# Row tiles and quadrants in the edge layers of a graph network kernel, and a node's own term moved out of the first stage

## The reference: two graph layers with residual and layernorm

```python
# first layer, a = node_vec1 (one number per node)
sc_s, sc_v = (xs @ Wsc0) * a/8,  (xv . Wsc1) * a/sqrt(32)      # a node's own term
f_s,  f_v  = (xs @ Wl1_0) * a/8, (xv . Wl1_1) * a/sqrt(32)     # gathered features
h = gelu(edge_attr_8 @ Wfc1 / sqrt(8))                          # [E, 64]
h = gelu(h @ Wfc2 / 8)                                          # [E, 64]
w0, w1, w2, w3 = split(h @ Wfc3 / 8)                            # [E, 192]
gs, gv = f_s[src], f_v[src];  y0, y1 = edge_attr_4[:, 0], edge_attr_4[:, 1:4]
mid = (w0*gs*y0,  w3*(gv . y1)/sqrt3,  (w1*gs) x y1,  w2*gv*y0)
m_s, m_v = segment_sum(mid, dst) / sqrt(32)
alpha = (m_s @ Wa) * a/sqrt(96)
out = (sc_s + alpha*(m_s @ Wl2_s)*a/sqrt(96),  sc_v + alpha*(m_v . Wl2_v)*a/sqrt(96))
x = layernorm(x + out)
```

## Time and profile before

| | us |
|---|---|
| median of 3 runs | 3056.2 |
| lowest and highest | 3023.99 and 3060.04 |
| the profiled execution's own time | 3079.29 |
| its span, first to last instruction | 3077.1 |

### The profile page before, as it was taken

One profiled execution on the slowest core, in us unless ns is written; L12 is line 12 of the kernel. 1 busy time (PEld: TensorE's weight loads), 2 busy tenths in 40 slices (PEclk: granted clock), 3 DMA queues, 4 the chain that ended last, 5 costly groups with the idle time before them and its releaser, 6 DMA issues.

```text
span 3077.1 us, 77590 instructions
## 1 busy us (share of the span) xinstructions
PE 2732.5 (89%) x24164; PEld 2006.0 (65%) x24164; DVE 1638.9 (53%) x4537; ACT 972.3 (32%) x2395; POOL 2004.7 (65%) x1630
## 2 busy tenths in 40 slices
PE   8768777887788888888899999999999999999996
PEld 4334434444444444444588888888888888888983
DVE  3446333443443443433466666666666666666664
ACT  2212212121121211121244444444444444444442
POOL 4555554554555555555188888888888888888884
PEclk5565666556655556665599999999999999999998
DMA  6233332232332332333278888888888887888887
GB/s 191 60 94 92 83 85 76 81 94 77 82 85 78 86 89 80 87 88 81 76 141 140 141 139 140 140 140 140 141 140 141 141 139 140 140 142 143 142 137 176
DMA packets 386447, 354.44 MB, mean 115 GB/s; under 512 B 60080, under 2 KB 337136, under 8 KB 386064
## 3 DMA queue, kind: packets, MB, share of 16 engines
q0 software_dynamic: 150528, 141.40, 31.9%
q1 hardware_dynamic: 231248, 206.49, 24.0%
q10 hardware_dynamic: 4544, 4.93, 0.6%
HBM read 244.83 MB, written 133.44 MB: 123 GB/s over the span
## 4 chain that ended last, share of the span: by engine, by line
PE 75%; another core or an unknown queue 12%; issue 6%; DVE 3%; ACT 2%; SPq 1%; DMA 1%; DVEq 0%; POOL 0%; ACTq 0%; POOLq 0%
PE ps_o L1043 11%; PE ps_w L1031 10%; PE ps_d L1052 8%; PE ps_o L1041 8%; PE ps_x L1065 6%; PE ps_w L894 6%; PE ps_h L887 5%; PE ps_h L882 5%; PE ps_p L838 5%; PE ps_x L1005 3%; PE ps_g L853 2%; PE ps_g L847 1%; PE ps_g L850 1%; PE ps_nd L910 1%
## 5 line engine op out<-in xcount | busy, mean ns | idle before, releaser
L620 POOL DMA_INDIRECT tab<-summed,sidx x784 | 1223.7, 1561 | 285.1 <-issue 229.1
L602 POOL DMA_INDIRECT gat<-f,gidx x784 | 751.8, 959 | 714.3 <-DVE feats L1350 409.6
L1490 DVE TENSOR_TENSOR prod<-ps_w,xg 128x768 f32<-128x768 f32 x392 | 375.5, 958 | 268.6 <-PE ps_w L1031 255.6
L1043 PE MATMUL ps_o<-ro_v,prod 128*128 128x96 f32 x3136 | 479.1, 275 | 0.0
L1043 PEld LDWEIGHTS ps_o<-ro_v,prod 128*128 128x128 f32 x3136 | 414.1, 192 | 0.0
L793 ACT ACTIVATE xg<-ps_x 128x768 f32<-128x768 f32 x392 | 296.4, 808 | 338.2 <-PE ps_x L1065 336.3
L887 PE MATMUL ps_h<-h,w 128*128 128x256 f32 x392 | 225.2, 675 | 178.9 <-issue 106.5
L1031 PE MATMUL ps_w<-hid,wf 64*128 64x128 f32 x4704 | 369.4, 290 | 2.0 <-ACT hid L794 2.0
L1041 PE MATMUL ps_o<-ro_s,prod 96*128 96x96 f32 x1568 | 328.0, 291 | 20.0 <-DVE msg L1501 6.8
L1031 PEld LDWEIGHTS ps_w<-hid,wf 64*128 64x128 f32 x4704 | 294.1, 187 | 70.3 <-issue 44.8
L1052 PE MATMUL ps_d<-msg,same 128*128 128x193 f32 x1568 | 332.3, 334 | 0.7 <-ACT summed L812 0.7
(11 more groups left out here) (259 smaller groups left out, 3330.0 us busy)
## 6 DMA issues: line engine op xcount, KB each, us to landing
xt<-in_src_rows SPq DMA_DIRECT2D x196, 256.0 KB
xt<-feat SPq DMA_DIRECT2D x784, 36.0 KB
xt<-in_ea SPq DMA_DIRECT2D x196, 128.0 KB
feat<-xt SPq DMA_DIRECT2D x25, 576.0 KB
hot_dst<-in_dst_rows SPq DMA_DIRECT2D x98, 128.0 KB
gat<-f,gidx POOLq DMA_INDIRECT x784
hot_dir<-sh_rows SPq DMA_DIRECT2D x98, 128.0 KB
xt<-hot_dst SPq DMA_DIRECT2D x196, 64.0 KB
```

Of the source, the lines that this page charges most:

```text
L602: pool.indirect_dma_start(out=gat[:, r % 4, k, :], out_offset=None, in_=t["f0"], in_offset=bass.IndirectOffsetOnAxis(ap=gidx[:, r // 4, at ...
L620: pool.indirect_dma_start(out=t["tabs"][into[k]], out_offset=bass.IndirectOffsetOnAxis(ap=sidx[:, r, k:k + 1], axis=0), in_=summed[:, r, k ...
L1043: last = pe.matmul(ps_o[:, k, 96 + 64 * c:192 + 64 * c], prod[:, ur % 2, k, 1 + c, :], ro_v[:, c, :], start=True, stop=True)
L1490: dve.tensor_tensor(prod[:, r % 2, :, :, :].rearrange("p k c e -> p k (c e)"), ps_w4[:, :, 0:3 * P], xg[:, r // 2, r % 2 * 2:r % 2 * 2 + 2 ...
```

## The change

Four parts. (1) Layer 1 takes two row tiles: 16 rows at partition 0 and 16 at partition 32, each with 128 columns, into two banks. (2) Layer 2 takes four 64x64 quadrants of 128 columns each, and the gelus are two instructions each; layer 3's order becomes 0, 2, 1, 3. To have the second bank, `ps_p` and both `ps_g` share one bank, and `tile_sums(u)` waits for `acc_done >= u`, the addition of the window sums of the group before. (3) The first stage multiplies by the weights of the gathered features alone, 64 and 96 columns, and DVE's additions are gone from it; the rows of x are loaded by SP, behind `y` and ahead of the first L399. (4) The own term is made in the first layer: two steps before a node tile's update its rows of x are turned (s mod 8 = 3), projected one step later with 64 and 96 columns (s mod 8 = 4), and added by DVE (`add_self`). The 25th tile's is made in step 3. The eight-column attributes lie in 48 rows of 128 columns a group instead of 16 of 256.

```diff
+SELF_LAST = 3
+def self_at(s, lag):
+    if s - lag == SELF_LAST:
+        return NT - 1
+    return tile_at(s, lag - 2, range(NT - 1))
...
-            w1 = sb(c2, "w1", [16, P])
+            w1 = sb(c2, "w1", [48, P])
-            ea8 = sb(c2, "ea8", [16, 2, 256])
+            ea8 = sb(c2, "ea8", [48, 2, P])
...
-            ps_h1, ps_h2 = ps_h[:, 0:256], ps_h[:, 256:512]
+            ps_hy = pb(c2, "ps_hy", [P, 512])
+            ps_h1 = [ps_h[:, 0:P], ps_hy[:, 0:P]]
+            ps_h2 = [ps_h[:, P:2 * P], ps_hy[:, P:2 * P]]
...
-            ps_p = pb(c2, "ps_p", [P, 512])
-            ps_gw = pb(c2, "ps_g", [P, 2, 256])
-            ps_g = [ps_gw[:, i, :] for i in range(2)]
+            ps_pg = pb(c2, "ps_pg", [P, 512])
+            ps_p = ps_pg[:, 0:FEAT]
+            ps_g = [ps_pg[:, FEAT + 4 * WIN * i:FEAT + 4 * WIN * (i + 1)] for i in range(2)]
...
                 for h in range(2):
-                    sp.dma_start(w1[8 * h:8 * h + 8, S * h:S * h + S], t["L0_gnn_Wfc1"]).then_inc(w_in, 16)
-                    sp.dma_start(w2[S * h:S * h + S, S * h:S * h + S], t["L0_gnn_Wfc2"]).then_inc(w_in, 16)
+                    for q in range(2):
+                        sp.dma_start(w1[32 * q + 8 * h:32 * q + 8 * h + 8, S * h:S * h + S], t["L0_gnn_Wfc1"]).then_inc(w_in, 16)
+                    for q in range(2):
+                        sp.dma_start(w2[S * h:S * h + S, S * q:S * q + S], t["L0_gnn_Wfc2"]).then_inc(w_in, 16)
                     sp.dma_start(w3raw[S * h:S * h + S, :], t["L0_gnn_Wfc3"]).then_inc(w_in, 16)
                 sp.dma_start(y[:, :, :], t["ea4"]).then_inc(y_in, 16)
+                for m in range(NC):
+                    sp.dma_start(xres[:, m * FT:(m + 1) * FT, :], t["x_rows"][:, m * FT:(m + 1) * FT, :]).then_inc(rows_in, 16)
...
-                    act.dma_start(xres[:, m * FT:(m + 1) * FT, :], t["x_rows"][:, m * FT:(m + 1) * FT, :]).then_inc(x_in[m], 16)
...
+                def self_turned(u):
+                    act.wait_ge(tr_done, turns_to_self(u))
...
+                    act.activation(xt2_s, ps_nd[0:S, 0:P], ACT.Copy)
+                    act.activation(xt2_v, ps_nd[0:96, P:2 * P], ACT.Copy).then_inc(xt2_done, 1)
...
-                    act.activation(h1[:, r % 2, :], ps_h1[:, :], ACT.Gelu_apprx_tanh,
-                                   scale=8.0 ** -0.5).then_inc(g1_done, 1)
+                    for q in range(2):
+                        last = act.activation(h1[:, r % 2, P * q:P * q + P], ps_h1[q], ACT.Gelu_apprx_tanh, scale=8.0 ** -0.5)
+                    last.then_inc(g1_done, 1)
...
-                    since(pe, res_ready, u - 5)
-                    parts_n = ps_n[u % 6][:, 0:2 * D].rearrange("p (k f) -> p k f", k=2)
                     here = slice(u * P, u * P + P)
-                    pe.matmul(parts_n[:, :, 0:S], xt_s[:, here], w_s2[:, :, :], start=True, stop=True)
-                    pe.matmul(parts_n[:, :, S:D], xt_v[:, here], w_v2[:, :, :], start=True, stop=True).then_inc(n_ready, 1)
+                    pe.matmul(ps_n[u % 6][:, 0:S], xt_s[:, here], w_s2[:, 0, :], start=True, stop=True)
+                    pe.matmul(ps_n[u % 6][:, S:D], xt_v[:, here], w_v2[:, 0, :], start=True, stop=True).then_inc(n_ready, 1)
...
-                    pe.matmul(ps_h1[:, :], w1[:, :], ea8[:, r, :], start=True, stop=True).then_inc(h1_ready, 1)
+                    for q in range(2):
+                        at = slice(32 * q, 32 * q + 16)
+                        last = pe.matmul(ps_h1[q], w1[at, :], ea8[at, r, :], start=True, stop=True)
+                    last.then_inc(h1_ready, 1)
...
-                    pe.matmul(ps_h2[:, :], w2[:, :], h1[:, r, :], start=True, stop=True).then_inc(h2_ready, 1)
+                    for c in range(2):
+                        for h in range(2):
+                            rows_h, cols_c = slice(S * h, S * h + S), slice(S * c, S * c + S)
+                            last = pe.matmul(ps_h2[h][cols_c, :], w2[rows_h, cols_c], h1[rows_h, r, P * c:P * c + P],
+                                             start=True, stop=True)
+                    last.then_inc(h2_ready, 1)
...
-                    for k in range(G):
+                    for k in (0, 2, 1, 3):
...
+                def project_self(u, turned, count, done):
+
+                    pe.wait_ge(turned, count)
+                    pe.matmul(ps_nd[:, 0:S], xt2_s, w_s2[:, 1, :], start=True, stop=True)
+                    pe.matmul(ps_nd[:, S:D], xt2_v, w_v2[:, 1, :], start=True, stop=True).then_inc(done, 1)
...
                             since(pe, part_done, u)
+                            since(pe, acc_done, u)
                             pe.wait_ge(sel_ready, u + 1)
                             pe.wait_ge(prod_done, u + 1)
                             tile_sums(pe, ur, part_ready)
...
+                        v = self_at(s, 0)
+                        if v is not None:
+                            if v == NT - 1:
+                                pe.wait_ge(rows_in, 16 * NC)
+                            else:
+                                pe.wait_ge(self_done, self_count(v) - 1)
+                                since(pe, y_done, v)
+                            turn(v, ps_nd, tr_done)
+                        v = self_at(s, 1)
+                        if v is not None:
+                            project_self(v, xt2_done, turns_to_self(v), self_ready)
...
-                for u in range(NT):
-                    dve.wait_ge(f_ready, u + 1)
-                    dve.scalar_tensor_tensor(xres[:, u, :], ps_n[u % 6][:, D:2 * D], a_col[:, u:u + 1], xres[:, u, :],
-                                             ALU.mult, ALU.add).then_inc(res_ready, 1)
...
+                def add_self(u):
+
+                    dve.scalar_tensor_tensor(xres[:, u, :], ps_nd[:, 0:D], a_col[:, u:u + 1], xres[:, u, :],
+                                             ALU.mult, ALU.add).then_inc(self_done, 1)
```

More of the change, by code:

```diff
@@ L120, in tile_at, with self_count, turns_to_self, turns_to_new @@
     return u - 1 if rest == 0 and u - 1 in tiles else None
+def self_at(s, lag):
+    if s - lag == SELF_LAST:
+        return NT - 1
+    return tile_at(s, lag - 2, range(NT - 1))
+def self_count(u):
+    return 1 if u == NT - 1 else u + 2
+def turns_to_self(u):
+    return 1 if u == NT - 1 else 2 * u + 2
+def turns_to_new(u):
+    return min(2 * u + 3, 2 * NT)
 def lagged(s, j, r, lag, unroll):
@@ L229, in gnn_kernel @@
             consts, ext_done, cnt_ps = (sem(cs, n) for n in ("consts", "ext_done", "cnt_ps"))
-            n_ready, f_ready, res_ready = (sem(cs, n) for n in ("n_ready", "f_ready", "res_ready"))
+            n_ready, f_ready, self_done = (sem(cs, n) for n in ("n_ready", "f_ready", "self_done"))
+            rows_in, self_ready = sem(cs, "rows_in"), sem(cs, "self_ready")
             zeroed, dv, rdv, win_set, src_set = (sem(cs, n) for n in ("zeroed", "dv", "rdv", "win_set", "src_set"))
@@ L699, in scale_outputs @@
                                            scale=inv * (2.0 ** -0.5 if cross else 1.0)).then_inc(ro_ok, 1)
+                def self_turned(u):
+                    act.wait_ge(tr_done, turns_to_self(u))
+                    if u == NT - 1:
+                        act.wait_ge(ext_done, 1)
+                    else:
+                        act.wait_ge(self_ready, self_count(u) - 1)
+                        since(act, y_ready, u)
+                    act.activation(xt2_s, ps_nd[0:S, 0:P], ACT.Copy)
+                    act.activation(xt2_v, ps_nd[0:96, P:2 * P], ACT.Copy).then_inc(xt2_done, 1)
                 def turned(u, bank):
-                    act.wait_ge(tr_done, u + 1)
+                    act.wait_ge(tr_done, turns_to_new(u))
+                    act.wait_ge(self_ready, NT if u >= NT - 2 else self_count(u))
                     since(act, y_ready, u)
@@ L744, in gelus @@
                     since(act, w_ready, u - 1)
-                    act.activation(h2[:, r % 2, :], ps_h2[:, :], ACT.Gelu_apprx_tanh,
-                                   scale=1.0 / 8.0).then_inc(g2_done, 1)
+                    for h in range(2):
+                        last = act.activation(h2[:, r % 2, P * h:P * h + P], ps_h2[h], ACT.Gelu_apprx_tanh, scale=1.0 / 8.0)
+                    last.then_inc(g2_done, 1)
                     if r % 4 == 0 and runs(u + 4, NGRP):
@@ L896, in layer3, with update @@
                     last.then_inc(w_ready, 1)
-                def update(u, bank, groups):
+                def update(u, bank, groups, own):
                     pe.wait_ge(acc_done, groups)
                     pe.wait_ge(r_ok, 6)
-                    if bank is ps_nd:
-                        since(pe, y_done, u)
+                    pe.wait_ge(self_done, own)
                     here = slice(u * P, u * P + P)
@@ L947, in step @@
                         if v is not None:
-                            update(v, ps_nd, groups_before(v))
+                            update(v, ps_nd, groups_before(v), self_count(v))
```

(18 more changed lines are left out.)

66 lines of the change are left out of this document (36 added, 30 removed).

## The result

The kernel after took 3100.4 us (median of 4, 3092.0 to 3115.5), the kernel before 3053.8 (4 runs). The difference of the medians is 47 us. The ratio of the two kernels is 1.0175, with a 95% interval of 1.0122 to 1.0228, which is 53 us. In a later measurement on another chip it was 1.0255 (1.0208 to 1.0302). My forecast was 2998 with a range of 2920 to 3085, so the time lies outside it on the slow side.

What follows compares the result with a forecast made beforehand. TensorE was taken to bound the first layer: 1274 us of low-clock work, less 130 for full clock, plus 267 idle. Terms -169 + 38 + 63 + 15 - 5 = -58 us gave 2998 us, range 2920 to 3085.

Steps and rivals of the forecast that it cites:

- The step that failed: First layer: shorter layers 1 and 2 cut each low-clock step from 6.02 to 5.14 us, saving 169 us.
- Rival B: First layer: saved TensorE time is waited out behind L738's delayed release, only the first stage counts; 3051 us, chance 0.18.
- C: First layer: slower through the DVE loop, 103 us of wait and 130 us of lost full clock; 3153 us, chance 0.12.
- A: First layer: DVE's addition moves ahead, so the new wait is hidden and its costs fall away; 2920 us, chance 0.17.
- D: Layer 2: the quadrants do not share the array, it stays at 1.15 us; 3082 us, chance 0.08.
- The own term: First layer: turning and projecting a node's own term costs 1.67 us for each of 23 tiles, plus 38 us.
- The new wait: Tile sums wait for DVE's window-sum addition: 0.75 us in bare steps, 63 us in all, bounds 34 and 103.
- The clock: First layer: waits in bare steps mean TensorE is granted less full clock; charged 15 us.
- First stage: Start: narrower projections save time, but SP's extra loads delay layer 1; -5 us, ends 0 and -16.
- Layer 3's order: First layer: the order 0, 2, 1, 3 changes nothing, as the row tiles already run side by side; 0 us.
- Gelus in two parts: ACT: splitting each gelu adds 0 to 0.38 us, covered by TensorE's other work; cost nothing.
- Instructions: TensorE: 16 more instructions per step, whose fetching was charged nothing.

Runs made afterwards that it cites:

- half_columns: Kernel before, but from the second edge group on layers 1 and 2 multiply only 128 of 256 columns; 1.0020 against before.
- wait_alone: Kernel before with one wait added: tile sums wait for the accumulator addition of the step before; 1.0028 against before, 9 us.
- the fillers: Kernel before with the shared bank, its wait and extra matmuls nobody reads in every step; 1.0393 with 256 columns, 1.0412 with the most filler.
- window_first: Kernel after with the own term added early, window sums ahead of layer 3 and their addition ahead of the products; 1.0040 against before, on the fast chip.
- own_early: Kernel after, but DVE adds the own term one of its steps earlier; 1.0160 against before, 49 us slower.
- l1_alone: Kernel before with only layer 1 in two row tiles, plus the shared bank and its wait; 0.9999 against before.
- incs_16: Kernel before with 16 semaphore increments on TensorE's queue ahead of each step's window sums, on the chip without late releases; 1.0999 against before, 263 us.
- incs_again: Kernel before with 16 semaphore increments on TensorE's queue ahead of each step's window sums, on a chip with late releases; 1.0319 against before, 98 us.
- l2_alone: Kernel before with only layer 2 in four quadrants, second gelu in two instructions, plus the shared bank and its wait; 1.0113 against before, 35 us slower.
- order_alone: Kernel before with only layer 3's order changed to 0, 2, 1, 3; 0.9984 against before.
- fill_1024: Kernel before with the shared bank, its wait and two unread 512-column matmuls per step, ahead of layer 2 and behind the window sums; 1.0412 against before, 127 us.

## Why the prediction was wrong

**The step that failed** is "So a step loses 0.88 us of TensorE time, from 6.02 to 5.14, and 192 steps lose 169 us". The durations were right (0.72 and 0.62 recorded for the 0.71 and 0.71 forecast). That the saved time would shorten the kernel was wrong: half_columns took the same columns away and gained nothing (1.0020). I had added up 1274 us of work, less 130 of clock, plus 267 of idle time, and then changed the first term as if the others stood still. They do not. The 130 us of clock were only what was left over to make the sum come out at 1411, so that it came out proved nothing. The recorded work and the idle time are two parts of one pace, 7.4 us a step (1490.3 less 52.9, by 195), in which releases come late; on the one chip without late releases it was 5.07. Rival B said this, at 0.18; the row for it, 243 us of L738's waits on "remote", was read and then set aside, because bare steps without idle time are common. An unnamed releaser of that size should have been the first suspect. In the chain of waits of before over 88 to 1499 us it has the largest share too, 24.5%; the next is layer 3 with 12.5%.

**The rivals.** B is right about the gain. It was too mild at 3051, as it let the new work be absorbed too, and it isn't. C forecast the right sign with its two terms, a wait in every step and lost full clock. Both are in the trace of after (171 us, clock 0.56), but the runs do not bear them out as the cause: wait_alone costs 9 us, and the fillers show that the pace stays far above the recorded work even at the full clock. A falls with the 169. D is wrong where releases are on time (window_first), and where they are late the missing gain is not the quadrants' alone, as half_columns has none of them.

**The own term** was put at +38. Alone it cost 56 us, on top of the edges 32. I missed a wait: DVE runs one step behind TensorE, so `add_self` comes behind the products of the same step, and the update one step later meets it by 64 us in sum. own_early removed that wait and the pace took it back.

**The new wait** was put at 63 us, in 72 bare steps. It appears in 132 steps and 171 us, since the layer 3 results that DVE needs are themselves late (its L1413 waits 140 us on "remote" in after). It costs 9 us (0 to 19) by itself, as TensorE would wait ahead of layer 2 otherwise.

**The clock** was put at 15. It did fall, 0.60 to 0.56, as it fell to 0.54 in half_columns; it is no plain measure of the work, though, since l1_alone has 0.63 with fewer columns than before. What the fall cost is not shown.

**First stage**: -5 was forecast, and layer 1 starts 9 us earlier. **Layer 3's order**: 0, and 0 measured. **Gelus in two parts**: 0 was forecast; no run has them alone, and the most that their longer time can cost is 12 us each. **Instructions**: "I see no row in which their fetching is the release of a wait, and charge nothing". There is none, and yet incs_16 and incs_again show that they are not free.

The loss in sum: the edge part costs 41 to 47 us, and l2_alone, with the quadrants, the second gelu in two parts and the shared bank's wait, 35 of them. The own term costs 32 more on top of the edges. The costs of the parts overlap: on the chip where the edges cost 41 and the own term 56, own_early, the whole change but for one wait, cost 49. The whole was 53 us by its ratio on the first chip and 79 on the last.

What stays open is what delays TensorE's results in all sessions but one. It isn't the wait, the order of layer 3, the number of columns or a low granted clock, since late releases stand in the traces of wait_alone, order_alone, half_columns and fill_1024 alike. What makes the quadrants cost time is open too, between their late results and their number of instructions.

## What to carry to other kernels

Before counting a shorter instruction as gain, look at what releases the waits of its consumers. A large share of "remote" or "issue" behind an engine that looks busy is a warning that its recorded times are not its pace, and halving the suspected work in a run that leaves it out tells in one measurement whether any gain can arrive. Replacing one full-array matmul by several that share the array paid in recorded time here, but not in the time of the kernel; where the columns were not the bound, only its price was left.

## What the runs showed of the hardware that I had not expected

- One program, two speeds: 2629 us in the one session on one chip, 3054 to 3092 in every other session, with nearly all of the difference in the first layer. In the slower sessions TensorE's results reach their consumers up to 10 us late, by the longest of the waits on "remote"; in the fast one no such wait is in the stretch shown.
- A semaphore increment on TensorE's queue cost 84 ns where releases come at the recorded ends and 31 ns where they are late.
- Filler matmuls raised the granted clock from 0.60 to 0.84 (fill_1024), and the time by 127 us.
- Four quadrants in place of one matmul shorten its record from 1.15 to 0.62 us, and l2_alone, which has them, took 35 us longer. Where releases are on time (window_first) the next engine starts within 0.1 us of that record's end.
